# A fused attention and mixture-of-experts kernel: the first SiLUs of the shared block ahead of the router's exponent, its second weight split inside the router, value products later in the attention loop, K padding later

## What is computed

```python
x = x + xattn0(layernorm(x), ctx)     # 16 heads of 16, q/k/v products, softmax over 361 keys, Wo
x = x + ffn0(layernorm(x))            # 8 experts of width 1024, top 2 with a capacity, and:
#   shared = silu(x @ sw1 + sb1) @ sw2 + sb2 ; out = y + 0.1 * shared
#   gates = softmax(x @ router_w); two rounds of argmax; positions by cumulative sums
x = x + xattn1(layernorm(x), ctx)     # ternary weights (sign, threshold by the mean of |W|), int8 inputs
x = x + ffn1(layernorm(x))            # a gated recurrence over 16 steps, then tanh
```

## Time and profile before

| | us |
|---|---|
| median of 3 runs | 918.67 |
| lowest and highest | 918.64, 931.78 |
| the profiled execution | 917.04 |
| its span | 915.10 |

### The profile page before, as it was taken

How to read it: one execution, slowest core, us unless ns; L and a number is a source line. 1 busy time by engine, 2 the same in 40 slices (tenths; PEclk the granted TensorE clock), 3 DMA queues, 4 the chain that set the end, 5 groups by cost and what they waited for, 6 DMA issues and landing times.

```text
span 915.1 us, 21761 instructions
## 1 busy us (share of the span) xinstructions
PE 775.8 (85%) x8198; PEld 584.1 (64%) x8198; DVE 702.4 (77%) x1455; ACT 557.9 (61%) x1156; POOL 291.6 (32%) x256
## 2 busy tenths in 40 slices
PE   3788999999998677899899999996647998869995
PEld 1456666666665464778477777783224886459994
DVE  7767888888888897876667776647886987767766
ACT  6657767677674346543655556646977775763542
POOL 6244544535442524050522220005721221532400
PEclk9789999999999778999999999999558999789997
DMA  6434444445543356242477766532210000200002
GB/s 174 109 75 101 118 100 108 108 107 125 140 106 90 94 189 227 90 128 58 125 200 192 197 194 175 151 89 60 74 37 1 1 1 10 85 0 3 3 1 72
DMA packets 75661, 89.60 MB, mean 98 GB/s; under 512 B 22069, under 2 KB 62276, under 8 KB 75584
## 3 DMA queue, kind: packets, MB, share of 16 engines
q1 hardware_dynamic: 68752, 80.50, 31.9%
q0 software_dynamic: 6144, 7.42, 3.3%
q10 hardware_dynamic: 688, 0.66, 0.3%
HBM read 72.87 MB, written 15.43 MB: 97 GB/s over the span
## 4 chain that ended last, share of the span: by engine, by line
PE 50%; DVE 20%; ACT 9%; issue 8%; POOL 6%; DMA 5%; SPq 1%; DVEq 0%; ACTq 0%; POOLq 0%
PE ps L1213 11%; PE ps L1200 9%; PE ps L575 4%; PE ps L547 3%; PE ps L475 3%; PE ps L528 3%; ACT area L1738 2%; PE ps L377 2%; PE ps L619 2%; PE ps L2298 2%; DVE p L563 2%; PE ps L2309 2%; PE ps L1814 2%; ACT area L1705 1%; DVE m L533 1%
## 5 line engine op out<-in xcount | busy, mean ns | idle before, releaser
L533 DVE TENSOR_REDUCE m<-ps 100x2 f32<-100x722 f32 x128 | 114.9, 899 | 48.1 <-PE ps L528 46.8
L554 ACT ACTIVATE p<-ps 128x800 f32<-128x800 f32 x128 | 106.6, 833 | 47.6 <-PE ps L547 45.7
L1262 ACT ACTIVATE hT<-ps,cols 128x500 f32<-128x500 f32 (+1 forms) x96 | 62.5, 651 | 96.6 <-PE ps L1200 85.8
L563 DVE SCALAR_TENSOR_TENSOR p<-p 128x600 f32<-128x600 f32 x128 | 106.1, 829 | 1.0 <-ACT p L554 1.0
L1213 PE MATMUL ps<-w_h,hT_h 128*125 128x256 f16 (+1 forms) x384 | 104.7, 273 | 1.8 <-DVE x L1309 1.2
L1213 PE MATMUL ps<-w_h,hT_l 128*125 128x256 f16 (+1 forms) x384 | 104.7, 273 | 0.0
L1213 PE MATMUL ps<-w_l,hT_h 128*125 128x256 f16 (+1 forms) x384 | 104.7, 273 | 0.0
L1269 DVE TENSOR_TENSOR hT_l<-hT,hT_h 128x500 f16<-128x500 f32 (+1 forms) x96 | 62.4, 652 | 54.6 <-ACT hT_h L1263 54.3
L1105 POOL DMA_INDIRECT xe<-tokens,slot_of x32 | 44.4, 1387 | 146.3 <-PE ps L1223 99.0
L1200 PE MATMUL ps<-xe_h,w_h 128*128 128x500 f16 (+1 forms) x192 | 71.4, 372 | 16.0 <-ACT hT_h L1263 6.2
L1200 PE MATMUL ps<-xe_l,w_h 128*128 128x500 f16 (+1 forms) x192 | 71.1, 370 | 0.0
(11 more groups left out here) (356 smaller groups left out, 2099.7 us busy)
## 6 DMA issues: line engine op xcount, KB each, us to landing
stage<-in_ctxT_dram SPq DMA_DIRECT2D x16, 541.5 KB, 6.2
sw<-in_L_ffn_w_dram SPq DMA_DIRECT2D x16, 512.0 KB
sw<-in_L_ffn_w_dram SPq DMA_DIRECT2D x8, 1024.0 KB, 5.9
k_parts<-kp SPq DMA_DIRECT2D x32, 192.0 KB, 3.9
ks<-k_parts SPq DMA_DIRECT2D x32, 192.0 KB
stage<-in_L_xattn_W_f_dram SPq DMA_DIRECT2D x6, 1024.0 KB, 7.7
ctx_f<-in_ctxT_dram SPq DMA_DIRECT2D x16, 270.8 KB, 3.1
ks<-k_parts SPq DMA_DIRECT2D x32, 96.0 KB
```

The costliest lines, as they stand in the source:

```text
L533: v.tensor_reduce(m32[p][:, 2 * i:2 * i + 2], ps[0:T, at:at + 2, 0:KV], AX.X, ALU.max).then_inc(m_max, 1)
L554: s.activation(p32[:, i % HALF, :, :, :].rearrange("p j n t -> p n j t"), ps[:, t_bank(i):t_bank(i) + 2, 0:(KJ + 1) * T].rearrange("p n (j ...
L563: v.scalar_tensor_tensor(probs, probs, 1.0, low, ALU.min, ALU.max).then_inc(a_cv, 1)
L1262: s.activation(hT[:, f % 3, 0:m], bank[2 + f % 2][:, 0:m], ACT.Silu, bias=bias, scale=1.0 / WS)
```

## The change

```diff
--- before
+++ after
@@ a_tensor @@
+                if i == 1 and has(b, 2):
+                    v_tensor(pe, b + 1, q, 0, (k_32, 2 * b + 5))
                 if i == 1:
                     pe.wait_ge(m_l, 2 * b + 2)
                 if i == 1 and from_(b, 1):
                     pv_tensor(pe, b - 1, q, NQ - 1)
-                if i == 1 and has(b, 2):
-                    v_tensor(pe, b + 1, q, 0, (k_32, 2 * b + 5))
...
-                if i == 5 and has(b, 1):
+                if i == 6 and has(b, 1):
                     pe.wait_ge(m_l, 2 * b + 3)
-                if i == 5:
+                if i == 6:
                     pv_tensor(pe, b, p, 1)
@@ opening_vector @@
             turn_vector(v, 0, 0)
-            for part in range(2):
-                second_vector(v, 0, 0, part)
 
             def fill(at):
-                if 5 <= at < 5 + FC:
+                if 5 <= at < 9:
                     low_vector(v, 0, 0, at - 5)
-                if at == 5 + FC:
+                if at == 9:
                     turn_vector(v, 1, 1)
+                if 10 <= at < 14:
+                    low_vector(v, 0, 0, at - 6)
+                if at in (14, 16):
+                    second_vector(v, 0, 0, (at - 14) // 2)
@@ prologue, DVE @@
             v.memset(ks_flat[0][32:64, :].bitcast(F32), MINUS_ONES).then_inc(k_pad, 1)
-            v.memset(ks_flat[0][64:128, :].bitcast(F32), 0.0).then_inc(k_pad, 1)
             v.memset(floor_k[:, :].bitcast(F32), 0.0).then_inc(k_pad, 1)
             split_weight(v, "Wk")
             open_stats(v, 0)
             open_norm(v, 0)
+            v.memset(ks_flat[0][64:128, :].bitcast(F32), 0.0).then_inc(k_pad, 1)
             split_weight(v, "Wq")
@@ opening, ScalarE @@
+            for f in range(3):
+                silu_scalar(s, 0, 0, f)
             s.wait_ge(r_exp_in, 1)
             s.activation(hit[:, :, :], logit[:, :, :], ACT.Exp).then_inc(r_exp, 1)
-            for f in range(FC):
+            for f in range(3, FC):
                 silu_scalar(s, 0, 0, f)
-            turn_scalar(s, 1, 1)
+                if f == 4:
+                    turn_scalar(s, 1, 1)
@@ prologue, SyncE @@
+            for c in range(CC):
+                k_store(sp, 0, 0, 0, c)
             sp.wait_ge(k_pad, 3)
             sp.dma_start(floor_k[ROW_M:128, :], a["pick_h"][:, H * AP:]).then_inc(floor_in, 16)
-            for c in range(CC):
-                k_store(sp, 0, 0, 0, c)
             k_load(sp, 0, 0, 0)
```

## The result

The changed kernel takes 959.64 us (957.38 to 963.41, 4 runs) where the kernel before, run beside it, takes 920.08. The ratio is 1.0444, 95% interval 1.0414 to 1.0475: slower. The forecast was 942.5 in 932 to 948. The direction is right, the size is not, and the result lies outside the range. The profiled execution took 959.26 us, its span is 956.7, 41.6 more than before.

The account below looks back on a forecast made before the run. TensorE was busiest, but three places where it waits were taken as the limits the change touches. Terms 22.3 + 1.5 + 0.6 - 0.3 = 24.1 us on 917.04 gave 941.1, 942.8 with the median; forecast 942.5, range 932 to 948.

Parts of the forecast that it names:

- term 1: FFN opening: the second weight split ends later and delays the stage load queued behind it; +22.3 us, +17 to +26.
- the dear 4.34: FFN opening: costly end for the second split w_l, 4.34 us as before the change, where 2.35 was taken.
- term 2: TensorE's clock in the FFN: lower after its idle from 365 to 389 us; +1.5 us, between 0 and 2.5.
- term 3: Attention loop: waits for m_low give way to others; +0.05 us a batch, +0.6 us in all, from -14 to +3.
- It gives back 0.05: Attention loop: with t(6) and s(6) ahead of pv, exp 6 starts little later and s(6) is done; saves 0.05 us.
- the first move: Attention loop: next batch's value product goes ahead of the m_low wait, but waits for ScalarE's K; 0.1 us more.
- term 4: Prologue: second memset of ks leaves DVE's queue head but returns before Wq's split; -0.3 us, from -1.3 to +1.
- The norm ahead of it can come only about 1 us sooner: Prologue: norm before the moved memset gains only about 1 us, since ScalarE still waits for the second context.
- that the loop gives its waits back: Rival, attention loop: all 14.2 us of m_low waits go, giving 927.7 us; 9%.
- that the loads hold the path less: Rival, FFN opening: the 18 us from split's release to stage load's landing shrink to 12, giving 936.5 us; 7%.
- that no load is late: Rival, FFN opening: SiLUs come earlier, router later, nothing behind them is delayed; 917 to 920 us; 2%.
- the last rival: Rival, FFN: TensorE's clock stays low through slices 5 to 7 and after the idle, w_l takes 4.34; 949.5 us; 8%.

Follow-up runs that it names:

- e5: Kernel before with only the FFN opening changed, plus two stage loads and the tokens' stores queued ahead of second_load(0) and the expert biases; 918.10 us, ratio 0.9981.
- e6: Kernel before with the opening's changed order on ScalarE and DVE, but the second split still ahead of the router; 919.04 us, ratio 0.9993.
- e4: Kernel before with only the opening changed: three SiLUs before the exponent, second split behind router steps 14 and 16; 947.27 us, ratio 1.0274.
- e10: e4 plus 22 repeats of a hidden product (132 unused matmuls) on TensorE while it waits for the third stage sum; 940.25 us, ratio 1.0260.
- e2: Kernel before with one loop move alone: pv(b, 1) in step 6, behind t(6) and s(6); 931.30 us, ratio 1.0118.
- e3: Kernel before with only the prologue changed: second memset of ks behind the norm, K's stores ahead of floor_k's load; 922.68 us, ratio 1.0012.
- e7: Kernel before with only SyncE's queue reordered: two stage loads and the tokens' stores ahead of second_load(0) and the biases; 918.44 us, ratio 0.9966.
- e11: e2, with DVE clipping only a third of each pair's exponents in batches 0 and 1; 921.67 us, ratio 1.0038.
- e14: Kernel before with pv(b, 1) moved to step 6, but between t(6) and s(6) instead of behind both; 921.20 us, ratio 1.0037.

## Why the prediction was right and wrong

- **Opening, term 1**: right, in mechanism and size. Forecast 22.3 us; the landing moved by 37.0 us, and 13.9 of it is the later end of the loop, so 23.1 are the opening's, and e5 and e6 show that it is this link. Reckoned from the last o_scalar, 13.9 us later than before, Exp ended at 353.1 and not at 351.7, since slices 0 to 2 ran at the lower clock almost to their end (0.50 from 350 to 360 us, 0.60 from 360 to 365) and the forecast had slice 2 at the full one; w_l ended at 369.1 against 368.4; from release to landing 18.1 us against 17.99. w_l took 2.21 us and not the dear 4.34, with nothing on GpSimd beside it (0.00 us busy from 380 to 385), and that agrees with the rule of the Trainium skill, page "SBUF — State Buffer", section "Who interferes with whom". Exp's table loads at 365.36, behind the SiLU that ends at 365.34; the drain of about 1.38 us that the Trainium skill, page "ScalarE: Activation LUTs", section "What ACT_TABLE_LOAD costs", adds to a switch is not in this trace either.
- **Clock, term 2**: the mechanism was right, the term was mis-sized. Forecast 1.5 us. The changed kernel's rest grew by 27.7 - 23.1 = 4.6 beyond the wait, of which 3.7 are in the three rows of TensorE above; e4 lost 8.8 against e10, a high value. I took the loss of two windows after an idle of 3.67 us for that after one of 24 us. The windows of e4 show what else there can be: a whole window at 0.50 behind the long idle, and another some 20 us later, which I had not priced. In the changed kernel both are shorter (0.50 until 405 us and 0.66 from 405 to 410; 0.66 from 425 to 430).
- **Loop, term 3**: wrong, and this is where the forecast failed. Forecast 0.6 us, measured 12.9, and 10 in the runs with the moves alone. Of the 12.9, 3.2 us are in batch 1 (19.75 against 16.54), 4.6 in the nine steady batches (16.90 against 16.39 us each) and 4.0 in the last two. The step that failed is "It gives back 0.05". It compared the new order with batch b = 6, whose wait in step 5 was 0.86 us. Of the ten batches from 111 to 259 us the other nine had 0.50 to 0.72 there, and the group of waits I had in hand says 14.2 us in 26, 0.55 in the mean. So exp 6 came 2.40 us behind exp 5 in my batch and 2.08 in a usual one; in the new order it is 2.45 (e2 and the changed kernel), near the 2.35 that I had worked out for it. The working was nearly right for the new order and wrong in what it was compared with: against a usual batch it would have given +0.27 us a batch, where 0.37 was measured, and not -0.05. The longer row of s, pv and y (0.18 us a batch) was not in my working, nor was GpSimd held up beside DVE in the first batches (5.0 us of waits up to 95 us where before had 2.4), nor the two last batches. For the first move the forecast was 0.1 us a batch, and the mechanism was right (the wait changes its name to ScalarE's K, 4.7 us); in batch 6 TensorE's step 2 comes 3.06 us after s(1) instead of 2.88, 0.18 more.
- **Prologue, term 4**: forecast -0.3, not told from nothing (e3). Its step "The norm ahead of it can come only about 1 us sooner" held (1.3 us), but the norm then took 3.12 us and not 1.38, and open_low began at 22.07 where I had it at 20.3.
- **The rivals and the signs**: that the loop gives its waits back was wrong in sign; that the loads hold the path less fell with 18.1 us; that no load is late fell with e4. The clock stayed low longer than forecast, as the last rival had it behind the idle, but w_l did not take the 4.34 us that this rival needed. Of the signs, the split, the table loads and the landing came as named; "the batch stays at 16.4 us" did not (16.90).
- **The sum**: 24.1 us forecast, 41.6 measured in the span. Of the 17.5 between them 12.3 are the loop's, 3.1 the clock's, 1.3 the prologue's (not told from nothing) and 0.8 the opening's. No rival named a loop that loses more than its 3 us, and that is why the range ended at 948.

## What to carry to other kernels

Before moving an instruction, list what stands behind the semaphore it gives, in every queue: here one 2.2 us split held two loads that nothing tied to it, and reordering the queue took the whole loss of the opening back. In a loop, price a new order against the group of waits over all batches and against the smallest of them, not against the one batch whose rows are on the page. An order that only trades one wait for another of a tenth of a microsecond more gains nothing and, by the rows, pays the tenth in every batch.

## What the runs showed that I had not expected

- GpSimd's subtraction of 361 elements takes 0.8 to 1.9 us in most places, and 3.1 or 4.6 us where DVE works without a break beside it; it ended 0.6 to 0.75 us behind the start of the first break (e2, e7, e11). Reductions from PSUM stood between the clips of the row that held it up (e2), but in e11 it ended beside such a reduction, so whether they hold it up too is open, as is the cause itself.
- The same matmuls of t, s, pv and y took 0.18 us longer in another order (e2 against e7), and the period followed (e14).
- A kernel with 22.7 us (an estimate: 132 matmuls at 0.17 us) of useless matmuls had a rest of its profile shorter by 8.8 us than the one that waited instead (e10 against e4), and by 6 to 7 us than the two others that waited.
